# Second layer of a graph transformer: message rows made first, projections beside the first gathered blocks, one loop for attention and graph part

## The reference, cut to what matters

```
xn = layernorm(x)
msg = xn * rsqrt(out_degree)            # one row per node
agg = segment_sum(msg[src], dst)        # 100000 gathered rows, 3125 sums
graph = elu((agg * rsqrt(in_degree)) @ weight + bias)
q, k, v = phi(xn @ Wq), phi(xn @ Wk), xn @ Wv      # phi(x) = x + 1 or exp(x)
kv = sum over all nodes of k (x) v                  # linear attention, 8 heads
att = (q . kv / z) @ Wo + bo;  h = LN(xn + att);  mix = LN(h + relu(h @ W1) @ W2)
x = x + graph + mix
x = x + experts(layernorm(x))           # best 2 of 8, rows sorted by expert
```

## Time and profile before

| | us |
|---|---|
| median of 3 runs | 4180.82 (4166.93 to 4185.86) |
| profiled execution, its time | 4171.07 |
| its span | 4169.2 |
| first layer, up to its experts | 1702 |
| first layer's experts | 306 |
| first pass of the second layer, no gathers of messages | 220 |
| 25 blocks gathered, mixers and graph parts beside them | 1414 |
| last two graph parts to the experts | 124 |
| experts and last sums | 403 |

### The profile page before, as it was taken

One profiled execution on the slowest core, in us unless ns is written; L12 is line 12 of the kernel. 1 busy time (PEld: TensorE's weight loads), 2 busy tenths in 40 slices (PEclk: granted clock), 3 DMA queues, 4 the chain that ended last, 5 costly groups with the idle time before them and its releaser, 6 DMA issues.

```text
span 4169.2 us, 37130 instructions
## 1 busy us (share of the span) xinstructions
PE 2651.2 (64%) x10229; PEld 2060.8 (49%) x10230; DVE 1104.8 (26%) x3439; ACT 471.6 (11%) x1011; POOL 2287.6 (55%) x1996
## 2 busy tenths in 40 slices
PE   0666664587878787588534657675665756437880
PEld 0444443476667676476323445454444544335660
DVE  4433322324242311100333323323313323220001
ACT  0000000100101011122111101010000100002220
POOL 0777776477777740000114777767777777720005
PEclk9888886777777766799767878787687776758995
DMA  4434435334333320221223343434334333312224
GB/s 118 121 105 108 109 97 155 114 80 109 79 102 92 96 61 13 60 64 50 91 95 109 77 109 85 108 76 125 99 92 112 85 102 95 94 53 72 86 63 126
DMA packets 355006, 384.25 MB, mean 92 GB/s; under 512 B 179145, under 2 KB 282168, under 8 KB 354863
## 3 DMA queue, kind: packets, MB, share of 16 engines
q0 software_dynamic: 237216, 252.87, 24.2%
q1 hardware_dynamic: 99162, 111.30, 8.2%
q10 hardware_dynamic: 18485, 18.45, 1.5%
HBM read 304.70 MB, written 75.80 MB: 91 GB/s over the span
## 4 chain that ended last, share of the span: by engine, by line
POOL 43%; PE 22%; issue 14%; DMA 7%; another core or an unknown queue 6%; DVE 2%; POOLq 2%; ACT 1%; ACTq 1%; SPq 1%; DVEq 0%
POOL xg L558 40%; PE bank L655 20%; DMA rows_b<-arena 4%; DMA xg<-feat,idx_cur 2%; PE bank L661 1%; POOL sorted_in L591 1%; POOL arena L604 1%; DMA agg_s<-agg_rows 1%; ACT arena L1076 1%; POOLq L549 1%; SPq L365 1%; DMA feat<-arena 1%; POOLq L548 0%; POOL xg L604 0%
## 5 line engine op out<-in xcount | busy, mean ns | idle before, releaser
L558 POOL DMA_INDIRECT xg<-feat,idx_cur x1600 | 1963.2, 1227 | 631.5 <-issue 435.1
L655 PE MATMUL bank<-xg,oh 125*125 125x256 f32 (+1 forms) x3324 | 966.6, 458 | 731.7 <-DMA xg<-feat,idx_cur 516.1
L655 PEld LDWEIGHTS bank<-xg,oh 125*125 125x125 f32 x3324 | 755.5, 232 | 933.9 <-DMA xg<-feat,idx_cur 550.9
L655 PE MATMUL bank<-arena,w_h 128*128 128x250 f32 (+1 forms) x1184 | 343.9, 440 | 44.8 <-ACT arena L1076 30.0
L655 PEld LDWEIGHTS bank<-arena,w_h 128*128 128x128 f32 x1184 | 228.5, 204 | 157.3 <-issue 103.8
L655 PE MATMUL bank<-arena 125*125 125x25 bf16 (+2 forms) x1000 | 229.5, 389 | 118.0 <-DVEq L1682 92.7
L661 PE MATMUL bank<-ident,arena 125*128 125x125 f32 (+1 forms) x600 | 135.3, 341 | 247.4 <-remote 209.9
L655 PEld LDWEIGHTS bank<-arena 125*125 125x125 bf16 (+1 forms) x1000 | 220.8, 306 | 128.0 <-issue 124.3
L1362 DVE TENSOR_SCALAR oh<-iota,dst_cur,w_cur 125x125 f32<-125x125 f32 x800 | 229.6, 417 | 141.0 <-PE bank L655 137.7
L655 PE MATMUL bank<-w_exp,arena 128*125 128x256 f32 x1024 | 234.4, 385 | 21.4 <-remote 21.2
L661 PEld LDWEIGHTS bank<-ident,arena 125*128 125x128 f32 (+1 forms) x600 | 83.7, 172 | 292.0 <-issue 287.8
(11 more groups left out here) (253 smaller groups left out, 2321.5 us busy)
## 6 DMA issues: line engine op xcount, KB each, us to landing
xg<-feat,idx_cur POOLq DMA_INDIRECT x1600, 3.9
arena<-sorted_in SPq DMA_DIRECT2D x49, 250.0 KB
sorted_out<-arena ACTq DMA_DIRECT2D x47, 250.0 KB
rows_x<-arena SPq DMA_DIRECT2D x15, 625.0 KB
arena<-rows_b SPq DMA_DIRECT2D x5, 1875.0 KB
sorted_out<-zeros SPq DMA_DIRECT2D x11, 750.0 KB
w_exp<-in_L_ffn_Wd POOLq DMA_DIRECT2D x8, 1024.0 KB, 6.7
w_exp<-in_L_ffn_W POOLq DMA_DIRECT2D x16, 512.0 KB, 5.8
```

The costliest lines, as they stand in the source:

```text
L558: pool.indirect_dma_start(xg[:, s, 0:D], None, feat, bass.IndirectOffsetOnAxis(ap=idx_cur[g % 2][:, s:s + 1], axis=0)).then_inc(xg_full[k] ...
L655: return pe.matmul(o, w, r, start=first, stop=last, skip_group_check=not check)
```

## The change

- POOL: one transfer (`h_big`, 25 x 256 numbers a partition, 3.2 MB) loads all rows of x while the first layer's experts run. The 25 transfers of expert results are issued at once, into `xg` (`y_big`), not five per step into `y`. Gathers follow when the five stores of messages have landed.
- DVE: `nodes1(s)` for all five steps: complete x, normalize into `n_big`, messages into one of two buffers `msg`.
- SP: five stores of messages; then all of x and all of xn in two transfers (3.2 MB each) to `rows_b`; then the weights for the second pass. DVE begins `project1(0)` when those two have landed (`nodes_stored`), for `row_a` overlays `h_big`.
- PE, DVE, ACT: `project1(s)` now holds `aggregate(s)`, for blocks 0 to 4.
- Second pass: four rounds of a mixer with aggregates at the places 1, 2, 3 and a graph part with one at its start; then a mixer with 0, 1, 2, 3 and a graph part with none. x stays in SBUF from the mixer to the graph part (no store and reload).
- `t4` gets a tile of its own, and `agg_s` becomes a cut of `arena`.

```diff
-FOUR, TWO, AG = (0, 2, 3, 4), (2, 3), 3
-AC = 2 * len(FOUR)
-AP = len(TWO) + AG
-AR = NB - AC - AP * (NS - 2)
+MIX, MIX_LAST = (1, 2, 3), (0, 1, 2, 3)
+AP = len(MIX) + 1
...
+        h_big = x_big
+        n_big = cut(6400, 6400).rearrange("p (b d) -> p b d", b=NB)
+        y_big = xg[0:B, 0:NB, 0:D]
+        msg = [cut(12800 + 1280 * j, 1280).rearrange("p (i n) -> p i n", i=G) for j in range(2)]
...
@@ block.sync
-            def project1(s, more):
-                take(sp, rowb_full)
-                sp.dma_start(rows(rows_b[:, 0:2 * D], s), row_b[:, :, 0:2 * D]).then_inc(rowb_free, 16)
-                take(sp, fout_full)
-                sp.dma_start(rows(feat1, s), f_out).then_inc(fout_free, 16)
-                if more:
-                    residual(s + 1)
-                take(sp, q_full)
...
+            for s in range(NS):
+                sp.wait_ge(msg_full, s + 1)
+                sp.dma_start(rows(feat1, s), msg[s % 2]).then_inc(msg_stored[s % 2], 16)
+            sp.wait_ge(nodes_full, NS)
+            sp.dma_start(by_part(rows_b[:, 0:D]), h_big).then_inc(nodes_stored, 16)
+            sp.dma_start(by_part(rows_b[:, D:2 * D]), n_big).then_inc(nodes_stored, 16)
...
-                sp.dma_start(f_out, rows(rows_x, s)).then_inc(aggs_in, 16)
+            nodes_in(0)
+            with sp.Fori(0, NS - 1) as p:
+                aggregates_in(p)
+                nodes_in(p + 1)
+                result_out(p)
+            aggregates_in(NS - 1)
+            result_out(NS - 1)
@@ block.gpsimd
+            pool.wait_ge(rowx_free, 16)
+            pool.dma_start(h_big, by_part(rows_x)).then_inc(rowx_in, 16)
...
-            collect(0, 0, (y,))
-            with pool.Fori(1, NS) as s:
-                collect(s, 0, (y,))
-                feat1_landed()
+            for i in range(NB):
+                pool.indirect_dma_start(
+                    y_big[:, i, :], None, sorted_out,
+                    bass.IndirectOffsetOnAxis(ap=pos_tab[:, 0, i:i + 1], axis=0)).then_inc(step_got[i // G], 16)
+            for j in range(2):
+                pool.wait_ge(msg_stored[j], 16 * ((NS + 1 - j) // 2))
+            for b in range(NB):
                 gather(1, b, feat1)
-                if b < AC + AP * (NS - 2) and (b - AC) % AP == 0 or b >= AC + AP * (NS - 2):
+                if b >= NS + AP + 1 and (b - NS - 1) % AP == 0:
                     scatter(2, row_a[:, :, D:2 * D])
             scatter(2, row_a[:, :, D:2 * D])
@@ block.tensor
-            def project1():
-                take(pe, v_full)
-                turn_rows(row_b[:, :, D:2 * D])
+            def project1(s):
+                pe.wait_ge(nodes_full, s + 1)
+                turn_rows(n_big[:, G * s:G * s + G, :])
...
+                aggregate(s, D + 1, 1, total)
                 take(pe, phi_full)
...
-            with pe.Fori(0, 2) as s:
-                mixer(s * len(FOUR), FOUR)
-            with pe.Fori(0, NS - 2) as p:
-                mixer(p * AP + AC, TWO)
-                graph(p * AP + (AC + len(TWO)), AG)
-            graph(NB - AR, AR)
+            with pe.Fori(0, NS - 1) as p:
+                mixer(p * AP + NS, MIX)
+                graph(p * AP + (NS + len(MIX)), 1)
+            mixer(NB - len(MIX_LAST), MIX_LAST)
             graph(NB, 0)
@@ block.vector
+            def nodes1(s):
+                at = slice(G * s, G * s + G)
+                h, n = h_big[:, at, :], n_big[:, at, :]
+                dve.wait_ge(rowx_in, 16)
+                dve.wait_ge(step_got[s], 16 * G)
+                for i in range(G):
+                    last = stt(out=h[:, i, :], in0=y_big[:, G * s + i, :], scalar=p_tab[:, G * s + i:G * s + i + 1],
+                               in1=h[:, i, :], op0=ALU.mult, op1=ALU.add)
+                chain(last)
+                norm(n, h)
+                dve.sem_inc(nodes_full, 1)
+                if s >= 2:
+                    dve.wait_ge(msg_stored[s % 2], 16 * (s // 2))
+                iv = inv_out[:, at].unsqueeze(2).to_broadcast([B, G, D])
+                chain(tt(msg[s % 2], n, iv, ALU.mult))
+                dve.sem_inc(msg_full, 1)
...
+            for s in range(NS):
+                nodes1(s)
+            onehots(0, False)
+            dve.wait_ge(nodes_stored, 32)
...
+            with dve.Fori(0, NS) as s:
+                project1(s)
```

More of the change, by code:

```diff
@@ L449, in _ @@
             sp.dma_start(bg_bc[:, :], row(a["L1_ffn_bg"])).then_inc(l_c, 16)
-            with sp.Fori(1, NS - 1) as s:
-                project1(s, True)
-            project1(NS - 1, False)
+            with sp.Fori(0, NS) as s:
+                take(sp, q_full)
+                sp.dma_start(rows(rows_b[:, 2 * D:3 * D], s), q1).then_inc(q_free, 16)
             take(sp, loop_b_done)
@@ L1134, in layer0, with project1 @@
                     step_ready()
-            def project1(more):
+            def project1(s):
                 copy_turned(2)
@@ L1150, in _ @@
             experts(0, J0, lambda e, j: b1_col[:, j:j + 1])
-            root(sd[:, :])
-            with act.Fori(0, NS - 1):
-                project1(True)
-            project1(False)
+            with act.Fori(0, NS):
+                root(sd[:, :])
+            with act.Fori(0, NS) as s:
+                project1(s)
             act.wait_ge(l_c, 16 * 7)
@@ L1682, in project1 @@
                 dve.sem_inc(phi_full, 1)
-                if more:
-                    norm0()
                 take(dve, q_free, 16)
                 take(dve, act_out2[0])
-                chain(stt(out=row_b[:, :, 2 * D:3 * D], in0=row_a[:, :, 0:D], scalar=0.0, in1=ek[:, :, 0:D],
+                chain(stt(out=q1, in0=row_a[:, :, 0:D], scalar=0.0, in1=ek[:, :, 0:D],
                           op0=ALU.max, op1=ALU.add))
                 dve.sem_inc(q_full, 1)
-                if more:
-                    messages1(s + 1)
                 chain.restart()
+                tails(s, False)
+                onehots(s + 1, False)
             onehots(AA * NS, True)
@@ L1737, in _, with mixer @@
             dve.wait_ge(l_bc, 16 * 7)
-            def mixer(b, stages):
+            def mixer(b, stages, more):
                 def hots(i):
@@ L1811, in graph @@
                           op0=ALU.max, op1=ALU.add))
-                chain(stt(out=f_out, in0=row_a[:, :, 0:D], scalar=-1.0, in1=f_out, op0=ALU.add, op1=ALU.add))
+                take(dve, fout_free, 16)
+                chain(stt(out=f_out, in0=row_a[:, :, 0:D], scalar=-1.0, in1=x1, op0=ALU.add, op1=ALU.add))
                 dve.sem_inc(fout_full, 1)
@@ L1832, in graph @@
                 positions(s, (lt[:, :, :], lu[:, :, :]))
-                if n and not isinstance(b, int):
+                if n:
                     onehots(b + n, False)
                 chain.restart()
-            onehots(0, False)
-            dve.sem_inc(rowx_used, 1)
-            with dve.Fori(0, 2) as s:
-                mixer(s * len(FOUR), FOUR)
-            with dve.Fori(0, NS - 2) as p:
-                mixer(p * AP + AC, TWO)
-                graph(p, p * AP + (AC + len(TWO)), AG)
-            graph(NS - 2, NB - AR, AR)
+            dve.sem_inc(aggs_used, 1)
+            with dve.Fori(0, NS - 1) as p:
+                mixer(p * AP + NS, MIX, True)
+                graph(p, p * AP + (NS + len(MIX)), 1)
+            mixer(NB - len(MIX_LAST), MIX_LAST, False)
             graph(NS - 1, NB, 0)
-            take(dve, rowx_used)
             routes(2)
             experts(1)
-            dve.sem_inc(got_used[1], 1)
+            dve.sem_inc(rowx_used, 1)
+            for j in range(2):
+                dve.sem_inc(got_used[j], 1)
             def sum_step(p, j, first, last):
```

155 lines of the change are left out of this document (42 added, 113 removed).

## The result

| | before | after |
|---|---|---|
| median of 7 runs, us | 4173.97 (4166.93 to 4185.86) | 4202.06 (4196.15 to 4210.00) |
| span of the profiled execution, us | 4169.2 | 4208.2 |

The ratio is 1.0065, with a 95% interval of 1.0048 to 1.0081: slower by 28 us in the medians. The profiled execution of after is the slowest of its seven, so that the spans differ by 39.0 us.

What follows compares the result with a forecast made beforehand. POOL's issue bounds the kernel from 2228 to 3640, a chain through all engines elsewhere. Terms -150.6 + 34 + 8.2 + 84.5 + 15.1 + 2 + 4 = -2.8 us: span 4166, median 4178, range 4140 to 4213.

Steps and rivals of the forecast that it cites:

- the slower rival: Second pass: the step's sums come late, 24 us instead of 10 for the load, about +35, to 4215; chance 0.2.
- My own case: Whole kernel: the terms sum to -2.8 us, span 4166, median 4178, own range 4160 to 4200; chance 0.5.
- the graph part's absences: Second pass: PE's absences over graph parts stall POOL 28 + 28 + 22 + 6.5 = 84.5 us.
- the first gather: End of first pass: first gather of messages at about 2078, not 2228.6, a gain of 150.6 us.
- the end: Last mixer and graph part: 79 us where before took 76.4, counted as +2.
- the signs named: Included first gather 2078 (+-5); POOL idle 20 to 30 us behind blocks 9, 13, 17, under 10 behind 5, 21.
- the three that were to prove the prediction wrong: `nodes_stored` before 2130, PE's absence behind the graph's aggregate under 50 or over 75 us, or experts over 10 us late.
- PE may be away between two aggregates for 43.5 us: Second pass: PE absences up to 43.5 us cost POOL nothing; the longest before, 39.8 us, was free.
- the prediction's own absence of 65.2: Loop's graph part: PE away 43.9 + 11.9 + 9.3 = 65.2 us, from its aggregate through `kvd`.
- The stall in block 0: First projections: stores of x and xn at 89 GB/s take 72 us; POOL stalls 34 us, bounds 14 and 53.
- The Trainium skill's fit: Rival, first projections: stores at the chip's rate, 6.4 MB within 50 us, no stall, 4144; chance 0.05.
- Between block 4 and 5: Start of second pass: PE away 52 us for sums, biases, `row_b`, turning and `kvd`, 8.2 over 43.5.

Runs made afterwards that it cites:

- e1: Changed kernel with MIX = (0, 2, 3) for (1, 2, 3): a step's first aggregate comes right behind the ranks; 4145.07 us, ratio 0.9915 to before.
- e2: Changed kernel with POOL's `h_big` load issued behind expert 2's weights instead of ahead of the experts; 4192.77 us in one run.
- e4: Changed kernel with ACT's five square roots of the `nodes1` steps written out instead of looped; 4199.77 us in one run.
- e3: Changed kernel with `project1(0)` waiting for `h_big`'s store alone, `n_big`'s waited for behind the projections; 4178.0 us, ratio 1.0008 to before.
- e6: Changed kernel with the edits of e2, e3, e4, plus MIX = (0, 2, 4) and the graph part's aggregate behind the `wn` product; 4052.64 us, ratio 0.9688 to before.

## Why the prediction was wrong

The forecast was "no change", 4178 us; the result is slower by 0.65%, inside the range of 4140 to 4213, in a case to which 0.21 was given. It is not the slower rival that came: the step's sums are not late. PE's first turning of `agg_s` follows the aggregate's end by 0.4 us (2626.7, then 2627.08). My own case came, with its largest loss a third too small. The traces are 41.8 us apart from the forecast (+39.0 for -2.8): 33.3 of them are the graph part's absences, 12.5 the first gather, 4.6 block 5 and 3.9 the end, less 8.7 in block 0 and 3.8 in other blocks. Of the signs named, the first gather at 2078 (+-5) failed, POOL was idle 42 us and not 20 to 30 in blocks 9 and 13, and 11 and 15 us and not under 10 behind blocks 5 and 21. Of the three that were to prove the prediction wrong, none came.

**The failed step: "PE may be away between two aggregates for 43.5 us."** It was worked out as 51.5 - 4.5 - 3.5, with 4.5 us for how late PE ends a block's aggregate after POOL began the next, and 3.5 for PE's first quarter. Both numbers came from one place of the kernel before, and were not the longest that its trace had: "up to 5.3 elsewhere" is not so. Here is the start of its block 12 and PE's closing of block 11:

```profile
2884.36 1.29 POOL L558 DMA_INDIRECT xg<-feat,idx_cur  x1 [2.14 <-remote]
```

```profile
2895.85 0.50 PE L655 MATMUL bank<-zero_r,zero_w 1*128 1x257 bf16 x3
```

That is a lag of 12.0 us in the prediction's count, and blocks 4, 8 and 21 have 10 to 12 as well. They cost nothing there, for PE was then away only 8 to 36 us. In the changed kernel such a lag stands ahead of an absence of 50 to 67 us. In after and e1, per block that meets a long absence (lag: PE's end of the aggregate before, less POOL's start of the block; absence: from there to the next aggregate's first product; stall: length less 51.5, 61.0 or 68.1 us for one, two or three tails):

| kernel, block (tails) | lag | absence | stall | lag + absence - stall |
|---|---|---|---|---|
| after, 5 (1) | 6.5 | 51.8 | 14.1 | 44.2 |
| after, 17 (1) | 3.6 | 69.8 | 28.3 | 45.1 |
| after, 21 (1) | 9.9 | 50.1 | 14.7 | 45.3 |
| e1, 17 (1) | 3.6 | 52.7 | 11.3 | 45.0 |
| e1, 21 (1) | 10.3 | 50.1 | 15.2 | 45.2 |
| after, 9 (3) | 10.2 | 67.1 | 35.7 | 41.6 |
| after, 13 (2) | 10.1 | 67.0 | 35.7 | 41.4 |
| e1, 9 (3) | 9.6 | 51.6 | 19.9 | 41.3 |
| e1, 13 (2) | 10.1 | 50.2 | 18.8 | 41.5 |

The last column is nearly constant: 45 us for a block with one tail, 41.4 with more. For one tail it is, by the way it is made, 51.5 less PE's first quarter; that it is constant says that what ends each stall is that quarter, or the first tail. So the rule of the prediction holds, and its sizes were off.

*The lag* is 10 us ahead of blocks 9, 13 and 21, where blocks 7, 8, 12, 16 and 20 have about 6. It isn't that PE is late: in block 8 it has used three quarters when it waits 12.96 us for the last one to land. SP's, POOL's and PE's rows there, POOL's being the block's last main gather:

```profile
2608.11 0.28 SPq L459 DMA_DIRECT2D arena<-rows_b  x1
```

```profile
2612.22 1.21 POOL L552 DMA_INDIRECT xg<-feat,idx_cur  x1 [0.30 <-issue]
```

```profile
2619.77 6.95 PE L647 MATMUL bank<-xg,oh 125*125 125x257 f32 x18 [12.96 <-DMA xg<-feat,idx_cur]
```

The last quarter can be used 7.6 us after the last gather's issue. In blocks 8, 12, 16 and 20 of after that is 7.2 to 7.6 us, and in the others in which PE waits for it 4.1 to 4.4. Those four are the blocks in which SP issues the 1.92 MB load of the next mixer's rows 4 us before. The kernel before has 9.1 to 11.1 us where such loads stand beside the last gathers, and 4.2 to 4.4 mostly elsewhere. No run moved this load, so that it is the cause rests on these rows alone.

*The first quarter* takes 6.3 us and not 3.5: 3249.36 to 3255.69, in block 17's aggregate. The 3.5 was read where the clock that PE was granted was 1.00 and did not have what passes from PE's last product to POOL's next gather: in block 0 of after, also at 1.00, the two make 4.6 us (2166.78 to 2171.34). The rest goes with the clock. Windows at PE's return, before ahead of block 13's sum, then in after ahead of block 9's and block 17's:

```profile
2982.90:2986.60 3.70, 3.65 (x17) 3.17 (x18) 1.66 (x2) 0.00 (x0) 3.09 (x3) 1.00 0.32 71
```

```profile
2693.80:2697.00 3.20, 3.18 (x8) 2.52 (x9) 0.92 (x4) 0.00 (x0) 0.00 (x0) 0.50 0.00 0
...
3249.30:3252.00 2.70, 2.64 (x8) 2.15 (x9) 0.50 (x2) 0.00 (x0) 0.00 (x0) 0.64 0.00 0
```

PE came back from these absences, in which it works in short pieces and waits between them, at or near the lower of its two levels (1.2 GHz), and made 8 products in 3.2 us where it had made 17 in 3.7. Put into the prediction's own absence of 65.2, lag (0.5 us longer in its count) and limit make 34.4 us for blocks 9 and 13 where it had 28, and 14.6 for block 21 (absence 49.5) where it had 6.5; block 17, with its short lag, gets 24.2 where it had 22. That is 23 of the 33 us by which this term was too small, most of it by the lag.

**The absences** were 67.1, 67.0 and 69.8 us against 65.2, and 50.1 against 49.5; less 0.5 each, for the prediction's way of counting, that is 7 more of the 33. (With the 5.2 below they come to 35, since block 21 had 1.8 over its 51.5 in the kernel before too.) The order of work in the prediction is the one in the rows of PE, down to the 11.24 us ahead of the last turning (11.9 there). Block 16, which meets no absence but that over `w2m`, took 5.2 us more for its second tail. PE began its aggregate 30 us behind POOL, no later than before (34 us), but then waited 12.84 us for its last quarter, 5.04 before: it is one of the four blocks with the load. The prediction had nothing for it.

**The first pass.** The first gather came 16.5 us later than the 2078 of the forecast. 11.1 of them were there before the pass began: `nodes1(0)` starts at 2031.33 instead of 2020.27, and e2 puts 6.7 of it on `h_big`, for which +4 stood with an upper bound of 16; the rest isn't settled, and kernels without this edit vary by as much. 2.6 is in the steps: "a table load that later steps don't have, since nothing else uses ACT" is false. No other function comes between, and yet the loop loads a table each time; e4 shows that it is the loop and not the function. Its steps took 47.4 us in all for after's 51.6, so the other terms of a step were forecast a little too long. The last 2.8 are between the last message and the first gather, 11.5 us for 8.7.

**The stall in block 0** was right in its cause, as e3 shows, and 9 us too long. PE's aggregate 0 began at 2166.8, within 7 us of the forecast 2160, while POOL came 16 later. The stores were quicker than forecast: from the last message, made at 2082.9, to DVE's going on at 2155.68 is 72.8 us, and the forecast had 79.7 (2069.3 to 2149), 7.2 for the message and 72 for x and xn. It let the two stores begin with the gathers; in the trace SP issues the first at 2083.31, 11 us ahead of the first gather. The 7.0 MB, the last message with them, moved at some 97 GB/s. The Trainium skill's fit (page "DMA: Bandwidth & Descriptors", section "Anatomy of one DMA"), by which the stall would have been nothing, is given there for transfers that GpSimd issues; these stores, which SP issues, are far slower than it would have them.

**Between block 4 and 5** the absence was 51.8 us, predicted 52 (its terms add to 51.3), with `row_b`'s load in it; its stall is 4.6 over the forecast: the lag was 6.5 and not 4.5, and the first quarter took 7.3 us (2450.15 to 2457.43) and not 3.5, less 1.3 that block 5 had over 51.5 before. **Scatters**: as predicted. **The end**: the stretch from block 24's aggregate to the last ranks took 78.6 (79 predicted); 2.8 more are behind the ranks, where nothing was changed, and are left open.

Where did the gain of 134 us go, then, and 39 more? 25 into the stall that the same bulk store causes, 131 into PE's absences (three quarters of it over the graph part in the loop, where now one aggregate stands instead of three), 15 into scatters, and 2 into the rest. Most of the absences' part is the order of work and not contention: e1 and e6 move aggregates and no data, and get 57 and a further 48 us of it back. Contention may have a part in the rest: some 4 us of lag ahead of each of blocks 9, 13 and 21, the 5 us of block 16, and, in a way that no run tested, the stores' rate beside gathers.

## What to carry to other kernels

Where one engine is kept busy by another that returns to it only now and then, write down for each return the lag it starts from, the absence, and what must be done before the first buffer is free; the limit is on their sum, and a lag counts against the next absence. Read the lag in the very block that stands ahead of it: here it was 10 us and not 6 wherever a bulk load was issued beside the block's last gathers. Look for second waits inside the block (here the one buffer for tail rows), since they stand earlier than the one at its end and can't be filled with work that is issued later. Spread the returns evenly before a stage is made shorter: the same four aggregates in a step cost 28 to 36 us a round in one order (after), and in another (e6) one stall of 12.9 us in all four. In the changed kernel more time was lost there and in block 0 than had been taken off the front.

## What the runs showed of the hardware

- A square root in a loop of ScalarE loads its table in every round (1.28 us each, five of five in after), and once when the five are written out (e4). ACT's program has no other function in that loop. By the Trainium skill, page "ScalarE activation tables: per-element evaluation and per-set limits", section "Table sets in the compiler and the runtime", the compiler's back end places table loads block by block; the two traces agree, if a loop's body is such a block.
- The 3.2 MB load of 3125 rows took POOL 3.8 us to issue. Issued while 2 MB of zero rows were to be stored, it made the experts begin 6.7 us later than when it was issued behind the weights of expert 2 (e2); that it is the store of the zero rows which it slows was not tested by itself.
- TensorE's granted clock over POOL's blocks, a mean of stretches at either level, was 0.77 before, 0.74 in after, where PE is away longest, and 0.77 again in e6. The window of e6:

```profile
2089.00:3475.00 1386.00, 888.20 (x3295) 668.57 (x3296) 442.76 (x1465) 138.49 (x268) 1050.24 (x899) 0.77 0.39 102
```

The same matmuls kept PE busy 888.2 us there and 908.2 in after (the window further up).
